# Layer norm's mean moved to ScalarE, with new orders for all engines and a new PSUM bank table

## The reference

```
h = relu(layernorm(x)); x = x + L0(h, adj)
h = relu(layernorm(x)); x = x + L1(h, adj)
h = relu(layernorm(x)); x = x + L2(h, adj)
h = relu(layernorm(x)); x = x + L3(h, adj)
```

## Time and profile before

| | before |
|---|---|
| median of three runs | 1414.67 us |
| profiled execution, its own time | 1416.56 us |
| span of the profiled execution, first to last instruction | 1414.6 us |
| TensorE busy, share of the span | 1368.1 us, 97% |
| VectorE busy | 1270.0 us, 90% |
| ScalarE busy | 1053.9 us, 74% |
| GpSimd busy | 949.0 us, 67% |
| DMA engines, mean busy share on the data queue | 13.7% |

### The profile page before, as it was taken

How to read it: one execution, slowest core, us unless ns; L and a number is a source line. 1 busy time by engine, 2 the same in 40 slices (tenths; PEclk the granted TensorE clock), 3 DMA queues, 4 the chain that set the end, 5 groups by cost and what they waited for, 6 DMA issues and landing times.

```text
span 1414.6 us, 33539 instructions
## 1 busy us (share of the span) xinstructions
PE 1368.1 (97%) x8924; PEld 1249.5 (88%) x8924; DVE 1270.0 (90%) x5265; ACT 1053.9 (74%) x2345; POOL 949.0 (67%) x974
## 2 busy tenths in 40 slices
PE   7789999999999999999999999999999999999985
PEld 6678999999999999999999999999999999999975
DVE  6869999999999999999999999999999999999883
ACT  4556777877777887777887777788777788777664
POOL 5647666667766666866666776666686666677533
PEclk9889999999999999999999999999999999999997
DMA  4100111101111101111110111110111111011001
GB/s 127 31 28 27 38 38 54 53 24 44 52 37 52 52 23 46 50 52 37 52 46 28 44 52 37 52 52 22 44 52 52 37 52 44 30 44 37 31 31 53
DMA packets 75383, 62.15 MB, mean 44 GB/s; under 512 B 3013, under 2 KB 70985, under 8 KB 75338
## 3 DMA queue, kind: packets, MB, share of 16 engines
q1 hardware_dynamic: 75338, 61.63, 13.7%
HBM read 36.45 MB, written 16.78 MB: 38 GB/s over the span
## 4 chain that ended last, share of the span: by engine, by line
PE 92%; DVE 5%; issue 2%; ACT 1%; DMA 0%; POOL 0%; POOLq 0%; DVEq 0%; ACTq 0%; SPq 0%
PE ps L357 39%; PE ps L342 25%; PE ps L361 19%; PE ps L463 4%; PE ps L418 3%; DVE stats L1321 1%; DVE prod L1505 1%; DMA x_in<-in_x 0%; PE ps L619 0%; DVE h L1333 0%; DVE x L1468 0%; PE ps L615 0%; DVE x L1416 0%; DVE z L1461 0%; DVE el L1406 0%
## 5 line engine op out<-in xcount | busy, mean ns | idle before, releaser
L1100 POOL TENSOR_TENSOR x3n<-p,x 128x512 f32<-128x512 f32 x64 | 82.2, 1285 | 260.7 <-ACT p L853 260.7
L1060 POOL TENSOR_TENSOR hT_lo<-hT,hT_hi 128x512 fp32r<-128x512 f32 x126 | 161.3, 1302 | 56.8 <-ACT hT L795 42.1
L1040 POOL TENSOR_TENSOR rs<-var_e,neg_half 128x4 f32<-128x4 f32 x160 | 165.2, 1033 | 23.7
L774 ACT ACTIVATE p<-ps,rs 128x256 f32<-128x256 f32 (+1 forms) x256 | 136.6, 597 | 27.9 <-DVE sij L1422 27.6
L357 PE MATMUL ps<-wl_hi,h2T_hi 128*128 128x512 f32 (+1 forms) x512 | 148.5, 372 | 0.7 <-DVE x L1468 0.7
L342 PE MATMUL ps<-p,alT 128*128 128x256 f32 (+1 forms) x512 | 143.4, 383 | 0.5 <-DVE p L1446 0.5
L357 PE MATMUL ps<-wl_lo,h2T_hi 128*128 128x512 f32 (+1 forms) x512 | 132.3, 340 | 0.0
L361 PE MATMUL ps<-wl_hi,h2T_lo 128*128 128x512 f32 (+1 forms) x512 | 131.8, 339 | 0.0
L1321 DVE BATCH_NORM_STATS2 stats<-x 128x6 f32<-128x256 f32 x256 | 108.8, 425 | 5.7
L871 ACT ACTIVATE h3T_hi<-ps 128x512 fp32r<-128x512 f32 x64 | 38.3, 598 | 90.8 <-PE ps L463 86.9
L795 ACT ACTIVATE hT_hi<-ps,cols_sb 128x512 fp32r<-128x512 f32 x128 | 87.4, 683 | 21.8 <-PE ps L361 21.6
(11 more groups left out here) (188 smaller groups left out, 4604.9 us busy)
## 6 DMA issues: line engine op xcount, KB each, us to landing
x_in<-in_x SPq DMA_DIRECT2D x32, 512.0 KB, 3.4
out_x<-x SPq DMA_DIRECT2D x32, 512.0 KB, 3.2
adj_f<-in_adjT SPq DMA_DIRECT2D x32, 256.0 KB, 2.7
adj_m<-in_adjT SPq DMA_DIRECT2D x32, 256.0 KB, 2.9
adj_l<-adj_m SPq DMA_DIRECT2D x32, 256.0 KB, 2.4
vqk<-in_l_wk SPq DMA_DIRECT2D x3, 256.0 KB, 4.9
x<-in_w1T SPq DMA_DIRECT2D x1, 512.0 KB, 6.7
x<-in_w2T SPq DMA_DIRECT2D x1, 512.0 KB, 7.6
```

The costliest lines, as they stand in the source:

```text
L774: return act.activation(dst, src, ACT.Copy, scale=scale)
L1040: pool.tensor_tensor(rs[:, layer, :], var_e[:, layer, :], neg_half[:], ALU.pow).then_inc(done, G)
L1060: pool.tensor_tensor(hTs[1][:, hc, :], hT[:, hc, :], hTs[0][:, hc, :], ALU.subtract).then_inc(S["hT_lo"], 1)
L1100: pool.tensor_tensor(x3n[:, s], p0[:, s], x2[:, s], ALU.add).then_inc(S["x3_ready"], 2)
```

## The change

Three things are changed. (1) `late_ln3` calls `spread_about` in place of `centred`; the new step `late_centre` on ScalarE then writes `h` as a relu with the negated mean as bias, and counts `h3_ready`. A new semaphore, `nm3_ready`, links the two. (2) The bodies of TensorE, ScalarE, GpSimd, VectorE and SP have a new order; the computation in each step is the same. Some steps cross the border of a round: `front_att(0)`, `front_att(1)`, `mid_az(2)`, `mid_az(3)`, `late_ak` and `elu_exp(0)` now stand at the end of their own round instead of in the next one; `elu_low(1)`, `elu_high(1)`, `mid_ln2(1)` and `mid_low(0)` now stand in the next one instead of at the end. `opening` follows suit. (3) The bank table is new, and with it the waits for banks: some go, some come, and the setup products use other banks.

The diff, cut to its core: the lines `if r.has_...:` are left out, unchanged steps stand without a sign, and of the waits for banks only some are shown (those in `front_w1`, `mid_p2`, `front_w2` and `tail_turn`, in that order).

```diff
-BANK = {"u": (1, 2, 0, 3), "y": (1, 4), "s": (3, 4), "d": (2,), "c2": (5, 0), "b1": (0, 3), "att": (3, 5),
-    "h2": (7, 6), "p2": (4, 5, 6, 7), "p10": (6, 7, 5, 0), "b2": (4,), "z": (0, 1, 2, 3),
-    "ap": (4, 5, 6, 7), "az": (5, 4), "h3": (5, 7), "vqk": (3, 1, 2, 0), "ak": (1,),
-    "row": (2,), "turn": (1,), "yA": (3, 2), "hp": (2, 6)}
+BANK = {"u": (3, 6, 0, 3), "y": (0, 3), "s": (2, 3), "d": (0,), "c2": (6, 1), "b1": (1, 2), "att": (5, 2),
+    "h2": (5, 6), "p2": (4, 5, 6, 7), "p10": (7, 4, 6, 0), "b2": (5,), "z": (0, 1, 2, 3),
+    "ap": (3, 4, 5, 6), "az": (2, 7), "h3": (4, 7), "vqk": (4, 6, 7, 1), "ak": (6,),
+    "row": (4,), "turn": (6,), "yA": (4, 1), "hp": (1, 5)}
...
 def load_x(r):
-    wait(sp, S["h0_ready"], r.front(G))
     wait(sp, S["xb_ready"], r.front(G))
+    if not r.steady and r.i in (0, 1, 2,):
+        wait(sp, S["h0_ready"], r.front(G))
     sp.dma_start(x_in[:], group(x, r.i + 1)).then_inc(S["x_loaded"], 16)
...
 def hand_adj(r):
+    wait(sp, S["al_ready"], r.mid(G))
     wait(sp, S["ak_ready"], r.late(G))
-    if not r.steady and r.i in (GROUPS - 2, GROUPS - 1, GROUPS,):
-        wait(sp, S["al_ready"], r.mid(G))
...
-        hand_adj(past)
-        store(past)
         load_mask(past)
+        hand_adj(r)
+        store(r)
...
     if hc == 0:
-        wait(pe, S["yT_lo"], r.front(2))
+        wait(pe, S["yT_lo"], r.front(G))
+    elif hc == 3:
+        wait(pe, S["hT_hi"], r.front(1))
     pe.wait_ge(S["yT_copied"], r.front(G))
     split_product(bank("u", hc), lambda a, c: w1s[a][:, c, hc * P:(hc + 1) * P],
                   lambda b, c: yTs[b][:, c, :], KC,
...
-    if g == 2:
+    if g == 0:
+        wait(pe, S["wex_ready"], r.tail(G))
+    elif g == 2:
         wait(pe, S["h2T_lo"], r.mid(G))
     pe.wait_ge(S["h2T_copied"], r.mid(2 * (g // 2) + 2))
...
     if not r.steady and r.i == 0:
         pe.wait_ge(S["w2_ready"], 3)
     if g == 2:
-        wait(pe, S["wex_ready"], r.tail(G))
+        wait(pe, S["x2_ready"], r.mid(G))
     elif g == 3:
         wait(pe, S["hT_ready"], r.front(G))
...
 def tail_turn(r):
+    wait(pe, S["p2_copied"], r.mid(3))
     pe.wait_ge(S["wn_ready"], r.tail(G))
...
         front_w1(r, 0)
-        front_att(past, 0)
-        front_att(past, 1)
-        mid_az(past, 2)
-        mid_az(past, 3)
+        tail_row(r)
+        front_w1(r, 1)
+        front_w1(r, 2)
+        front_w1(r, 3)
         front_att(past, 2)
         front_att(past, 3)
-        front_w1(r, 1)
-        front_w1(r, 2)
-        late_ak(past)
         mid_h2(r, 0)
-        front_w1(r, 3)
+        front_w2(r, 1)
+        front_w2(r, 0)
+        front_w2(r, 3)
+        front_w2(r, 2)
+        front_w2_low(r, 0)
         mid_h2(r, 1)
+        front_w2_low(r, 1)
         mid_p2(r, 0)
         mid_p2(r, 1)
-        front_w2(r, 0)
-        front_w2(r, 3)
-        tail_row(r)
         mid_p2(r, 2)
-        front_w2(r, 1)
         mid_p2(r, 3)
-        front_w2(r, 2)
-        front_w2_low(r, 0)
-        front_w2_low(r, 1)
         front_w2_low(r, 2)
         front_w2_low(r, 3)
         front_sums(r, 0)
         front_sums(r, 1)
         front_sums(r, 2)
         front_sums(r, 3)
+        late_h3(r, 0)
         mid_b2(r)
-        late_h3(r, 0)
+        tail_turn(r)
         mid_p10(r, 0)
         mid_p10(r, 1)
         front_c2(r, 0)
         front_c2(r, 1)
-        tail_turn(r)
         front_c2(r, 2)
+        front_c2(r, 3)
         next_s(r, 0)
         next_s(r, 1)
-        front_c2(r, 3)
         mid_p10(r, 2)
...
         late_vqk(r, 0)
+        late_vqk(r, 1)
         mid_ap(r, 0)
         next_d(r)
         mid_ap(r, 1)
-        late_vqk(r, 1)
         front_b1(r)
         mid_ap(r, 2)
         mid_ap(r, 3)
+        late_vqk(r, 2)
         next_y(r, 0)
-        late_vqk(r, 2)
         late_vqk(r, 3)
         next_y(r, 1)
         mid_az(r, 0)
+        mid_az(r, 1)
+        mid_az(r, 2)
         front_mix(r, 0)
-        mid_az(r, 1)
+        mid_az(r, 3)
+        late_ak(r)
         front_mix(r, 1)
+        front_att(r, 0)
+        front_att(r, 1)
 def opening(r):
...
+def late_centre(r, b):
+    centre(3, x3n, h, b, r.late, S["nm3_ready"], S["h3_ready"])
...
         copy_u(r, 0)
-        elu_exp(past, 0)
-        relu_p0(past, 1)
+        copy_u(r, 1)
+        copy_u(r, 2)
+        copy_u(r, 3)
         elu_exp(past, 1)
-        copy_u(r, 1)
-        copy_u(r, 2)
+        square(r, 0)
+        square(r, 1)
         copy_h2T(r, 0)
-        copy_u(r, 3)
-        square(r, 0)
-        copy_h2T(r, 1)
-        square(r, 1)
         tail_exp(r)
+        copy_h2T(r, 1)
+        late_centre(r, 0)
+        late_centre(r, 1)
         copy_p2(r, 0)
         copy_p2(r, 1)
         copy_h3T(r, 0)
         exp_edges(r)
-        copy_p10(r, 0)
-        copy_p10(r, 1)
-        norm_x(r, 0)
-        copy_s(r, 0)
-        copy_s(r, 1)
-        norm_x(r, 1)
-        centre_logits(r, 0)
-        copy_h3T(r, 1)
-        copy_p10(r, 2)
-        centre_logits(r, 1)
-        copy_p10(r, 3)
         weigh(r, 0)
+        norm_x(r, 0)
+        copy_p10(r, 0)
+        copy_s(r, 0)
+        copy_p10(r, 1)
+        copy_s(r, 1)
+        centre_logits(r, 0)
+        copy_p10(r, 2)
+        centre_logits(r, 1)
+        copy_h3T(r, 1)
+        copy_p10(r, 3)
         copy_vqk(r, 0)
+        norm_x(r, 1)
+        copy_vqk(r, 1)
         weigh(r, 1)
-        copy_vqk(r, 1)
         front_centre(r, 0)
         leaky_part(r, 0)
...
         softmax(r, 0)
+        copy_vqk(r, 2)
         softmax(r, 1)
+        copy_vqk(r, 3)
         front_centre(r, 1)
-        copy_vqk(r, 2)
+        copy_h1T(r, 0)
+        keep_x3(r)
         copy_yT(r, 1)
-        copy_vqk(r, 3)
-        copy_h1T(r, 0)
-        keep_x3(r)
         copy_h1T(r, 1)
         relu_p0(r, 0)
+        relu_p0(r, 1)
+        elu_exp(r, 0)
 def l1_hi():
...
-        front_scale1(past)
-        add_bias(past, 1)
-        add_x4(past, 0)
         add_x4(past, 1)
+        add_xb(past, 1)
         add_res0(r, 1)
-        add_xb(r, 0)
         add_x3(past, 0)
+        front_lo(r, 0)
         add_x3(past, 1)
-        front_lo(r, 0)
         front_lo(r, 1)
         front_lo(r, 2)
         front_lo(r, 3)
+        add_squares(r, 0)
         mid_scale(r)
-        add_squares(r, 0)
         add_squares(r, 1)
         join_squares(r)
         next_scale(r)
+        front_scale0(r)
         shift_x(r)
-        front_scale0(r)
+        mask_edges(r)
         late_scale(r)
-        add_xb(r, 1)
+        front_scale1(r)
         add_bias(r, 0)
-        mask_edges(r)
+        add_bias(r, 1)
+        add_xb(r, 0)
+        add_x4(r, 0)
...
     dve.wait_ge(S["x3_ready"], r.late(2 * b + 2))
-    centred(3, x3n, h, b, r.late, S["st3"], S["ag3"], S["h3_ready"])
+    spread_about(3, x3n, b, r.late, S["st3"], S["ag3"], S["nm3_ready"])
...
         next_moments(r)
+        elu_low(past, 1)
+        next_count(r)
+        elu_high(past, 1)
+        mid_ln2(r, 1)
+        mid_low(r, 0)
+        late_ln3(r, 0)
+        mid_low(r, 1)
+        next_inverse(r)
+        late_ln3(r, 1)
+        mid_columns(r)
+        next_binc(r)
-        tail_sum(r)
-        mid_low(r, 1)
-        late_ln3(r, 0)
-        tail_max(r)
-        next_count(r)
-        next_inverse(r)
-        mid_columns(r)
-        next_binc(r)
-        late_ln3(r, 1)
+        tail_norm(r)
         front_variance(r)
-        tail_norm(r)
+        tail_out(r)
         late_low(r, 0)
         mid_edges(r)
         front_residual(r, 0)
-        tail_out(r)
+        front_residual(r, 1)
         front_ln1(r, 0)
-        front_residual(r, 1)
+        front_ln1(r, 1)
         next_degrees(r)
-        front_ln1(r, 1)
         front_dots(r, 0)
         front_dots(r, 1)
...
         front_leaky(r, 0)
+        mid_z1(r, 0)
+        front_max(r, 0)
+        mid_z1(r, 1)
         front_leaky(r, 1)
-        front_max(r, 0)
+        mid_z1(r, 2)
         front_max(r, 1)
-        mid_z1(r, 0)
-        mid_z1(r, 1)
         front_weights(r, 0)
+        mid_z1(r, 3)
         front_weights(r, 1)
         y_low(r, 0)
-        y_low(r, 1)
-        mid_z1(r, 2)
         front_low(r, 0)
-        mid_z1(r, 3)
         mid_vb(r, 0)
         mid_vb(r, 1)
-        next_penalty(r)
-        front_low(r, 1)
-        elu_low(r, 0)
+        y_low(r, 1)
         mid_vb(r, 2)
         mid_vb(r, 3)
+        tail_weights(ahead)
+        tail_sum(ahead)
+        elu_low(r, 0)
+        front_low(r, 1)
+        tail_max(ahead)
         elu_high(r, 0)
-        elu_low(r, 1)
+        next_penalty(r)
         mid_ln2(ahead, 0)
-        elu_high(r, 1)
-        mid_ln2(ahead, 1)
-        mid_low(ahead, 0)
-        tail_weights(ahead)
 def opening(r):
```

More of the change, by code:

```diff
@@ L427, in next_y @@
             def next_y(r, c):
[L428 to L430 removed]
+                if c == 1:
                     wait(pe, S["z1_ready"], r.mid(1))
@@ L482, in mid_p10 @@
                 if g == 0:
-                    wait(pe, S["p2_copied"], r.mid(3))
+                    wait(pe, S["p2_copied"], r.mid(G))
```

(36 more changed lines are left out.)

166 lines of the change are left out of this document (79 added, 87 removed).

## The result

The changed kernel takes 1417.89 us (median of 15 runs, 1417.21 to 1422.76), the kernel before 1416.06 in the same comparison (15 runs); the ratio is 1.0020, its 95% interval 1.0011 to 1.0028. So it is slower by 0.2%, about 2.8 us. The forecast was 1415.8 in a range of 1405 to 1426, with hardly more chance for slower (0.35) than for faster (0.33).

The account below looks back on a forecast made before the run. The prediction took TensorE, back to back in steady rounds, as the bound. It added +3.6 us for steady rounds and -2.5 for the first rounds and the end, +1.1 on 1414.67, giving 1415.8 (range 1405 to 1426).

Parts of the forecast that it names:

- the forecast's own signs: Listed observations: right meant a round about 42.0 waiting only before `front_b1`; wrong included over 5 us arising outside steady rounds.
- The new wait: TensorE before `front_b1` in each steady round, released by `wh12`: late by 0.24 us (0.18 to 0.30).
- The wait on VectorE's chain: VectorE from `mid_columns` to `front_columns`: `wh12` ready at 15.09, `front_b1` starting at 15.32 against TensorE ready at 15.08.
- inside the same slack: At `tail_turn`, which waits on the same chain some 12 us earlier: its delay was not added.
- The wait that goes: TensorE's `front_w2(2)` would no longer wait for `wex_ready`, 0.09 us less in each steady round.
- The rest, at nothing: Bank table, GpSimd's `add_bias`, `add_xb`, `add_x4` moved to its body's end, and SP's `x_in` load: no cost.
- Neither engine is the steady bound, so the term is 0: Mean subtraction moved from VectorE (0.78 us less a round) to ScalarE (1.98 more): taken as 0.
- The cover that I named: TensorE's two last low passes, the sums and `late_h3(0)`, while ScalarE's `copy_p2` stand behind `late_centre(1)`.
- The ends: First rounds and end of the run: fewer waits on TensorE, -2.5 us, bounds -7.1 and +2.9.
- VectorE's queue as the bound: Slower rival: VectorE decides through `mid_low(1)`, for which `mid_p2(2)` waits; 0.45 us a round, +10.1, 1424.8; chance 0.28.

Follow-up runs that it names:

- delay_in_chain: The changed kernel with two unread 128x128 copies added on VectorE behind `next_binc` in the steady rounds; 1425.56 us, ratio 1.0070 to the kernel before.
- turn_later: The changed kernel with `tail_turn` behind `mid_p10(0)` on TensorE and `tail_out` behind `late_low(0)` on VectorE; 1416.02 us, ratio 1.0000 to the kernel before.
- before_mean_act_late: The kernel before with only the fourth layer norm's mean moved to ScalarE, `late_centre(0)` behind `tail_exp`; 1410.90 us, ratio 0.9964 to the kernel before.
- pool_off_rz: The changed kernel with GpSimd's `add_xb(1)` made to wait until VectorE has scaled all four softmax weights; 1411.91 us, ratio 0.9982 to the kernel before.
- rz_one_input: The changed kernel with the product `rz` done by two VectorE instructions with one SBUF input and a per-partition scalar; 1418.06 us, ratio 1.0016 to the kernel before.

## Why the prediction was right or wrong

The time was right, by a sum whose terms were each about half of what they were: +3.6 for +7.0 in the steady rounds, -2.5 for -6.0 at the ends. That is luck, and the forecast's own signs say so. A difference of more than 5 us before the fourth round was to show it wrong; 7.2 had arisen by round 4. The new wait was to stand before `front_b1` and nowhere else; it stands at `tail_turn`, and another at `front_mix(0)`. VectorE's busy time fell by the 0.8 a round that was named (1270.0 to 1243.6 in all), ScalarE's rose by 1.3, not by 2 (1053.9 to 1095.0).

- **The wait on VectorE's chain: the right chain (delay_in_chain), the wrong place, and the size by luck.** I had `wh12` ready 15.09 after the end of `mid_p2(3)`; it came at 675.74 - 660.64 = 15.10. But 0.20 of that is the second `front_residual` waiting for `front_c2`, so the chain by itself takes 14.90. I had TensorE at `front_b1` by 15.08 and late by 0.24; without its 0.25 at `tail_turn` it would be there at 675.83 - 660.64 - 0.25 = 14.94. So the wait of 0.25 is another one than the 0.24 of the sum: it is that of `tail_turn` for the first part of the chain, up to `tail_norm`, which I had left out as lying "inside the same slack". `front_b1` finds `wh12` just in time, also in turn_later, where both come 0.12 earlier.
- **The wait that goes: sized too small.** `front_w2(2)`'s wait for `wex_ready` was 0.135 a round, not 0.09 (in before_mean_act_late the first pass of `front_w2(2)` takes 0.11 less and the pass ahead of it 0.03; every other product takes what it did).
- **The step that failed: "The rest, at nothing"**, where GpSimd's `add_xb` was priced by GpSimd's own time, "still off the path". Its second half, `add_xb(past, 1)` at the head of the next body, now runs beside `rz`, and VectorE stands still for 0.6 behind it: 0.20 to 0.21 of a round (pool_off_rz). In sum 0.25 + 0.21 - 0.135 = 0.325 where the rounds show 0.253; the missing -0.07 lies in the arrangement of the blocks, of which I have taken only the sums apart. A step from one kind of product to another can cost time: in the kernel before, the first two matmuls of a `late_vqk` take 0.55 behind `mid_ap` and 0.35 behind another `late_vqk`. By kind, from start to start over rounds 8 to 29, the new order saves most in `mid_p2` (0.20 with the 0.03 above), `front_att` (0.11), `mid_p10` and `late_vqk` (0.09 each) and loses nearly as much in `mid_az` (0.19 besides the wait for `rz`), the high and low passes of `front_w2` (0.17 besides the wait that goes) and the transposes of `h` (0.11).
- **"Neither engine is the steady bound, so the term is 0": wrong.** In the new order the move is worth 0.43 a round, in the old one 0.135: the instructions that VectorE no longer does stood ahead of `mid_low(1)` and of `tail_max`. The cover that I named, TensorE's low passes, was ScalarE's; VectorE's had none. The rule of the Trainium skill that I weighed ("ScalarE: Activation LUTs", Rules for kernel authors) holds for the instruction, 0.502 on ScalarE against 0.468, but says nothing of the queue that it leaves.
- **The ends: right in sign, too small.** -2.5 forecast, -6.0 in the profiles (-7.2 up to round 4, +1.2 behind round 31), of which some 3.2 is a stretch at half speed that not every execution need have. At the end TensorE waits longer for two layer norms: 3.19 in place of 1.69 ahead of the second `mid_h2` of the last round that has a middle stage (1367.72), and 2.38 in place of 1.61 ahead of the last `late_h3(0)`, where one more engine, ScalarE, now stands in the chain. Against it the wait for `wex` behind that falls from 1.83 to 0.28.
- **VectorE's queue as the bound** did not come: `mid_p2(2)` doesn't wait in the changed kernel. But it was near: `h2T_lo` is written at 659.04 and `mid_p2(2)` begins at 659.21, and in rz_one_input, where VectorE has a few more small instructions, 0.08 of waiting is there.

## What to carry to other kernels

An engine's busy share doesn't price a step; its place does. The same 0.28 us on VectorE cost all or nothing according to which side of one wait it stood on, and 0.39 taken from in front of a short reduction gained 0.135 a round on TensorE, which showed as fully busy.

When an engine off the path is reordered, look at what runs beside it on the engines that are on the path, not only at its own queue: a stretched small instruction (0.78 for 0.16) is the sign.

Compare two orders at points where the same amount of work is done; a difference of 1 us in the whole was here -7, +7 and +1.

## What the runs showed of the hardware

A VectorE product of two SBUF operands (128x2) that was issued while GpSimd's 128x512 addition ran took 0.75 to 0.86 us instead of 0.16 in the steady rounds (0.50 in one round of some runs), and ended with GpSimd's operation; with one operand in SBUF and the other factor as the scalar of each partition (in the form that also writes a sum) it took 0.21 beside the same addition. The kernel before has one such case too, 0.97 in the first round. The Trainium skill, "SBUF — State Buffer", section Who interferes with whom, states that: a VectorE instruction with two SBUF inputs contends with a GpSimd instruction that reads SBUF, and the later one waits for the whole of the earlier. The traces agree, and the forecast should have weighed the rule when GpSimd's steps were moved.
